# Big-head attention on one core: a wide subtraction as an entry of its own in the plan, and the statistics of three blocks one head earlier

## The reference, cut to what matters

```python
xn  = x / max(|x|, 1e-12) * sqrt(128) * gamma
q, k, v = split(xn @ w_qkv.T)            # 8 heads of width 128
sim = (q * 128**-0.5) @ k.T              # 2048 x 2048 for each head
sim = where(causal_mask, -max, sim)
out = softmax(sim) @ v                   # then @ w_out.T over all heads
x   = layernorm(x + out)
```

## Time and profile before

| | us |
|---|---|
| median of 3 runs | 1998.93 (1997.27 to 2002.44) |
| the profiled execution's own time | 2002.52 |
| its span | 2000.7 |
| TensorE busy | 1787.3 (89%) |
| VectorE busy | 1559.0 (78%) |
| ScalarE busy | 1374.9 (69%) |
| GpSimd busy | 419.6 (21%) |

### The profile page before, as it was taken

How to read it: one execution, slowest core, us unless ns; L and a number is a source line. 1 busy time by engine, 2 the same in 40 slices (tenths; PEclk the granted TensorE clock), 3 DMA queues, 4 the chain that set the end, 5 groups by cost and what they waited for, 6 DMA issues and landing times. The chain is left out here.

```text
span 2000.7 us, 40527 instructions
## 1 busy us (share of the span) xinstructions
PE 1787.3 (89%) x15880; PEld 958.9 (48%) x15880; DVE 1559.0 (78%) x2275; ACT 1374.9 (69%) x2569; POOL 419.6 (21%) x650
## 2 busy tenths in 40 slices
PE   6799999999999888849999999899679999998785
PEld 2122222222222278826888888789312322233384
DVE  5899999999999443547988788877578979785434
ACT  3499999999999743426665666566347998888331
POOL 4201000000000403343432221312320011122413
PEclk8599999999999988969999999999868999999597
DMA  5000000000000168700000000000100000000274
GB/s 171 1 3 4 4 11 3 4 11 4 4 11 5 34 220 279 243 21 1 1 1 1 1 1 1 1 1 1 55 1 2 5 4 11 5 12 7 67 264 154
DMA packets 52878, 81.57 MB, mean 41 GB/s; under 512 B 9200, under 2 KB 37744, under 8 KB 52560
## 3 DMA queue, kind: packets, MB, share of 16 engines
q1 hardware_dynamic: 47520, 70.50, 11.1%
q0 software_dynamic: 3072, 6.30, 1.0%
q10 hardware_dynamic: 2096, 2.17, 0.4%
HBM read 64.13 MB, written 12.06 MB: 38 GB/s over the span
## 5 line engine op out<-in xcount | busy, mean ns | idle before, releaser
L827 DVE TENSOR_REDUCE a_mx<-psum 128x2 f32<-128x1024 f32 (+2 forms) x832 | 906.0, 1154 | 75.3 <-PE psum L602 42.2
L753 ACT ACTIVATE a_cs<-psum 128x512 f32<-128x512 f32 (+3 forms) x1664 | 856.9, 571 | 80.7 <-PE psum L620 62.5
L643 PE MATMUL psum<-a_cs,a_V 128*16 128x256 f32 (+1 forms) x6400 | 501.7, 384 | 20.8 <-ACT a_OD L733 9.7
L602 PE MATMUL psum<-a_KS,a_QS 48*128 48x512 bf16 (+3 forms) x1664 | 328.7, 386 | 30.4 <-DVE a_mx L827 27.3
L620 PE MATMUL psum<-a_QS,a_KS 51*128 51x512 bf16 (+3 forms) x1664 | 336.8, 379 | 4.9 <-ACT a_cs L753 3.0
L620 PEld LDWEIGHTS psum<-a_QS,a_KS 51*128 51x128 bf16 x1664 | 87.8, 93 | 354.9 <-ACT a_cs L753 310.1
L2159 PE MATMUL psum<-b_VW,b_ST 128*128 128x129 f32 x2176 | 249.4, 276 | 0.3 <-DVE X L2291 0.3
L2159 PEld LDWEIGHTS psum<-b_VW,b_ST 128*128 128x128 f32 x2176 | 245.4, 192 | 0.5 <-DVE X L2291 0.5
L643 PEld LDWEIGHTS psum<-a_cs,a_V 128*16 128x16 f32 x6400 | 107.1, 94 | 245.1 <-issue 120.5
L2266 DVE TENSOR_TENSOR b_M<-b_M,b_ST 128x512 f32<-128x512 f32 (+3 forms) x264 | 158.1, 599 | 40.5 <-ACT b_ST L2198 11.8
L2203 ACT ACTIVATE b_ST<-b_ST 128x2048 f32<-128x2048 f32 x48 | 91.8, 1911 | 124.6 <-DVE b_ST L2274 124.6
(11 more groups left out here) (233 smaller groups left out, 1773.7 us busy)
## 6 DMA issues: line engine op xcount, KB each, us to landing
e_W<-in_l_experts SPq DMA_DIRECT2D x45, 576.0 KB, 5.8
e_W<-in_l_experts SPq DMA_DIRECT2D x21, 768.0 KB, 5.7
yg<-e_yout SPq DMA_DIRECT2D x14, 256.0 KB, 6.0
xg<-zeros SPq DMA_DIRECT2D x2, 1472.0 KB, 9.7
a_cs<-in_rope ACTq DMA_DIRECT2D x4, 512.0 KB, 10.0
a_QS<-a_mrow SPq DMA_DIRECT2D x128, 3.0 KB
a_cs<-in_rope SPq DMA_DIRECT2D x1, 2048.0 KB, 7.7
a_num<-a_OD SPq DMA_DIRECT2D x120, 16.0 KB
```

What stands on the lines that cost most here:

```text
L602: mm = pe.matmul(ps[:, 2 * slot + half, 0:width], QS[rows, 2 * p + i, q_cols(qb, qt * P, P)], KS[rows, 2 * p + i, c * BLK:c * BLK + width] ...
L643: mm = pe.matmul(ps[32 * j:32 * j + 2 * HD, AV_BANK, a:b], V[:, kt, HPP * p + j, :], probs(e, a, b), start=(kt == 0 and half == 0), stop=last,
L753: act.activation(probs(HPP * s + j, c, BLK), ps[:, plan.bank(entry), c:BLK], ACT.Exp, scale=scale).then_inc(exp_done, 1)
L827: dve.tensor_reduce(mx[:, pk % 2, qt, 2 * i:2 * i + 2, c], banks, AX.X, ALU.max).then_inc(max_done, 1)
```

## The change

`subtract` was one event for an atom, with all its wide and diagonal subtractions in a row. It becomes "narrow" events, one for each wide group and one for the four diagonal tiles, with due times 2.6 us apart. They stand in one sorted list, `timed`, with the exponentials. The first wide exponential is due 3.8 us behind the first subtraction, as before; each further one is now 2.6 instead of 2.3 us later. The diagonal exponentials were due at 1.5 + 2.3 (qb + 1) us (at least 4.0) and are now due 1.5 us behind the diagonal subtractions, at the earliest 0.1 us behind the last wide exponential. The statistics of the blocks 0 to 2 ("stats", VectorE) are due 10, 12 and 14 us behind the reduce of atom 26; "measure" stays for GpSimd's power, behind the reduce of atom 27.

```diff
-        self.clock, self.turns, self.spreads, self.norms, self.exps = 0.0, [], [], [], []
+        self.clock, self.turns, self.spreads, self.norms, self.timed = 0.0, [], [], [], []
...
         while self.norms and self.clock >= self.norms[0][0]:
             self.events.append(self.norms.pop(0)[1])
-        while self.exps and self.clock >= self.exps[0][0]:
-            self.events.append(self.exps.pop(0)[1])
+        self.due()
 
     def turn(self):
         _, a = self.turns.pop(0)
         self.events.append(("reduce", a))
+        if a == NORM_ATOM - 1:
+            behind = max(n for n, (qb, h) in enumerate(self.atoms) if qb in EARLY_BLOCKS)
+            self.norms = [(self.clock + 10.0 + 2 * n, ("stats", g, behind)) for n, g in enumerate(EARLY_BLOCKS)]
         if a == NORM_ATOM:
-            behind = max(n for n, (qb, h) in enumerate(self.atoms) if qb in EARLY_BLOCKS)
             for n, g in enumerate(EARLY_BLOCKS):
-                self.norms += [(self.clock + 0.5 + n, ("measure", g, behind)), (self.clock + (12.0, 14.0, 47.0)[n], ("normalize", g)),
+                self.norms += [(self.clock + 0.5 + n, ("measure", g)), (self.clock + (12.0, 14.0, 47.0)[n], ("normalize", g)),
                                (self.clock + (45.0, 48.0, 54.0)[n], ("fold", g))]
             self.norms.sort()
         self.spreads.append((self.clock + 4.5, a))
 
     def spread(self):
         _, a = self.spreads.pop(0)
-        self.events.append(("subtract", a))
         qb = self.atoms[a][0]
-        self.exps += [(self.clock + 1.5 + 2.3 * (g + 1), ("wide", a, g)) for g in range(qb)]
-        self.exps.append((self.clock + max(4.0, 1.5 + 2.3 * (qb + 1)), ("diagonal", a)))
+        for g in range(qb):
+            self.timed += [(self.clock + 2.6 * g, ("narrow", a, g)), (self.clock + 2.6 * g + 3.8, ("wide", a, g))]
+        behind = self.clock + 2.6 * qb
+        self.timed += [(behind, ("narrow", a, qb)), (max(behind + 1.5, self.clock + 2.6 * (qb - 1) + 3.9), ("diagonal", a))]
+        self.timed.sort()
+
+    def due(self):
+        while self.timed and self.clock >= self.timed[0][0]:
+            self.events.append(self.timed.pop(0)[1])
...
-            while self.exps and self.exps[0][1][1] <= a:
-                self.events.append(self.exps.pop(0)[1])
+            while any(event[1] <= a for _, event in self.timed):
+                self.events.append(self.timed.pop(0)[1])
...
-                def subtract(a):
+                def subtract(a, g):
                     qb = plan.atoms[a][0]
-                    dve.wait_ge(row_done, a + 1)
-                    dve.wait_ge(max_done, plan.max0[a + 1])
-                    for g in range(qb):
+                    if g == 0:
+                        dve.wait_ge(row_done, a + 1)
+                        dve.wait_ge(max_done, plan.max0[a + 1])
+                    if g < qb:
                         group = ST[:, plan.at[a][g], :, :]
                         dve.tensor_tensor(group, group, row[:, a % 2, :].unsqueeze(1).broadcast_to([P, TPB, BLK]),
                                           ALU.subtract).then_inc(wide_sub, 1)
+                        return
                     for i in range(TPB):
...
-                    elif event[0] == "subtract":
-                        subtract(event[1])
+                    elif event[0] == "narrow":
+                        subtract(event[1], event[2])
...
-                    elif event[0] == "measure":
+                    elif event[0] == "stats":
                         dve.wait_ge(added, 2 * (event[2] + 1))
                         norm.variance(dve, chain, event[1])
```

More of the change, by code:

```diff
@@ L1968, in lay @@
                     self.emit(("product", a, kt, half), 0.265 * len(self.columns(a, kt, half)))
-        assert not self.norms and not self.exps
+        assert not self.norms and not self.timed
         self.ring = [event for event in self.events if event[0] in ("query", "score", "fold")]
```

## The result

| | before | after |
|---|---|---|
| median, measured side by side (6 runs each) | 2001.18 (1997.27 to 2002.94) | 2010.88 (2004.58 to 2013.18) |
| ratio | | 1.0044, 95% interval 1.0029 to 1.0058 |
| the profiled execution's own time | 2002.52 | 2012.82 |
| its span | 2000.7 | 2011.0 |

The change makes the kernel 0.44% slower, 9.7 us in the medians. The forecast, +3.4 us, had the sign and not the size; 2010.88 lies 2.9 us above the top of the range, 2008.0. Of that, 2.3 us is that the kernel before came out at 2001.18 here and not at 1998.93; the rest is in the terms.

A forecast was written before the change was run, and what follows sets the result against it. TensorE was taken to wait for short VectorE instructions (b_GL) queued behind long ones; -0.6 - 0.3 + 2.9 - 2.0 + 3.4 = +3.4 us on 1998.93 gave a median of 2002.3, range 1993 to 2008.

The forecast's parts named there:

- term 4: Atoms 25 to 31: subtractions still fit before the next query, b_GL late by nothing; 0, at most 0.2 once or twice.
- term 3: Atom 24: b_GL comes 1.69 us earlier, the wait of 3.12 shrinks to 1.5; gain 2.0 us.
- Term 2: Atoms 18 to 23 (block 2): diagonal exponentials ahead of ScalarE's copy of tile 0 delay tile 5; 2.9 us slower.
- The rival with the full length: Block 2: tile 5 waits the exponentials' full 1.45 us all six times, 8.7 instead of 2.9; total 2008.1; chance 0.12.
- the one with nothing: Block 2: the exponentials cost nothing, term 2 is 0; total 1999.4 us; chance 0.16.
- Term 1: Small atoms: b_GL earlier by four diagonal subtractions, part lost to exponentials ahead of copies; gains 0.6 and 0.3 us.
- the 4.1: Small atoms: rest of the 5.5 us query wait, taken as no gain; rival that they give it: 1998.2, chance 0.08.
- Term 5: Statistics ahead of query 28: new wait of 5.2 us there, a second at query 29; 3.4 us slower.
- The clock part: Term 5: low granted clock behind the two new waits; 2.6 us slower if one has it, at most 4.8 if both.
- the statistics hide: Query 29: the wait of 6.11 falls to some 0.4 with its 2.2 of clock; total 1991.0 us; chance 0.10.
- the rival: GpSimd's power: part of its 7.49 us was a wait for statistics, so normalize's 1.9 wait goes; 2000.4; chance 0.12.

The follow-up runs named there:

- f7: The kernel after, unchanged, timed again in a later series: 2008.45 us, ratio 1.0022 to the kernel before.
- f6: The kernel after with the diagonal exponentials due as before in block 3 alone: 2007.40 us, ratio 1.0025 to the kernel before.
- f5: The kernel after with the diagonal exponentials due as before in block 2 alone: 2002.01 us, ratio 0.9997 to the kernel before.
- e4: The kernel before with only the new due times of the exponentials, subtractions one entry: 2003.08 us, ratio 1.0001.
- g4: The kernel before with only the new due times of the exponentials, timed a second time: 2003.70 us, ratio 1.0016.
- g5: The kernel after with diagonal exponentials and statistics back at their old places, leaving the split of the subtractions: 1998.72 us, ratio 0.9992 to the kernel before.
- e1: The kernel after with the diagonal exponentials alone back at their old due times: 2000.47 us, ratio 0.9990 to the kernel before.
- e2: The kernel after with the statistics alone back behind the reduce of atom 27: 2008.76 us, ratio 1.0033 to the kernel before.
- e3: The kernel before with the statistics alone moved to behind the reduce of atom 26: 2001.14 us, ratio 0.9994.
- g9: The kernel before with one statistics block in each all-reduce gap of atoms 25 to 27, normalize of blocks 0 and 1 in atom 28's: 1996.03 us, ratio 0.9972.

## Why the prediction was wrong

**The step that failed is term 4**, "b_GL was late by nothing there", put at 0 and measured at 3.8 us (27.70, and 27.65 in f7, for 23.90). b_GL was not late, but near it. For query 27 TensorE was due at its tile 4 at 1241.41 + 3.76 = 1245.17 before, and b_GL ran from 1243.78 for 0.68: 0.7 us of slack. I looked at the two parts of the change one at a time and priced each at nothing. Together they move b_GL from 11.48 to 13.13 us behind the reduce of atom 25 (12.41 with the exponentials alone, 11.70 with the split alone; 0.93 and 0.22 do not add up to the 1.65). And the gain of term 3 had brought query 27 from 9.1 to 8.3 us behind that reduce, which uses up slack as well. So 1.65 + 0.8 - 0.7 = 1.75 late; measured is a wait of 1.91, with 0.88 of granted clock over 1250 to 1260, together +3.8 us at query 28. The table of four shows that it takes both parts; the split alone has 1.1 of it. f6 shows what the other 2.7 are worth: 2.7 us at their place and nothing that can be measured in the whole, since VectorE's own bound takes most of it back one query on. By whole runs the dearer part is block 2, where the interval of f5 (0.9988 to 1.0005) lies under that of f7 (1.0008 to 1.0036).

**Term 2 had the mechanism, and its own atoms nearly the size; what lay beside them was in no term.** The segment has 4.0 for the 2.9 forecast. The atoms of the term, 18 to 23, put their exponentials behind queries 20 to 25. These queries are 18.89 apart instead of 18.37, 2.6 us for the five, and query 25 to 26 is 0.5 longer: 3.1 in all, the same as in e4 and g4. At 1137.80 tile 4 comes 4.34 behind its query instead of 4.26, and tile 5 1.09 behind tile 4 (1143.23) instead of 0.77 (1141.47 before): the copy of tile 0 is late as said, by 0.32 for the 0.44 forecast, and the longer wait for b_GL comes on top. The other 0.95 lie between query 19 and 20, behind atom 17, which no term has. There too the split puts an accumulate between the wide subtractions, and b_GL waits for GH, by 1.57 instead of 0.84; TensorE waits 0.66 for it here, 0.32 with the split alone and not at all before:

```profile
1085.05 0.69 DVE L2243 TENSOR_TENSOR b_GL<-psum,b_GH 128x512 fp32r<-128x512 f32 x1 [1.57 <-ACT b_GH L2190]
```

This stretch takes 17.60 before and with the exponentials alone, 18.22 with the split alone and 18.55 with both: what term 4 overlooked at atom 25 was overlooked here as well. f5 takes 3.4 of the 4.0 away. The rival with the full length, 8.7, is out, and so is the one with nothing. That f5's median gains 6.4 on f7's where the segments show 4.2 stays open; the part outside the stage varies by more than that from one profile to another.

**Term 1 was right on the split and wrong on the exponentials.** The split alone is worth 2.1 us in the small atoms (g5 and e1), more than the 0.9 taken: of the 4.1 that I had put down to VectorE's total, some is to be had. The early diagonal exponentials cost 3 us there (e1 and g5 against e2, f5 and f6). The main place of it is ahead of query 3, where TensorE now waits 1.36 for ScalarE's copy of the values: query 2 to 3 takes 11.08 in all seven kernels with the diagonal exponentials late and 12.31 to 14.00 in the seven profiles with them early, of which the next stretch gives 0.35 back. I had counted only the scores' copies behind them.

**Term 3 was right**: 2.2 for 2.0, the wait 1.65 for 1.5, and the granted clock of 1220 to 1230 is 1.00.

**Term 5 had its waits, and no price.** The profile after has all of its parts: the statistics between the subtractions of atom 26, the b_GL of query 28 behind them, and normalize held up by GpSimd's power, 1.59 for a forecast of 1.9:

```profile
1266.97 0.86 DVE L942 BATCH_NORM_STATS2 b1n_stats<-X 128x6 f32<-128x128 f32 x4
...
1276.30 0.68 DVE L2243 TENSOR_TENSOR b_GL<-psum,b_GH 128x512 fp32r<-128x512 f32 x1
...
1300.88 1.12 DVE L1836 TENSOR_SCALAR big_raw<-X,b1n_mv,b1n_scales 128x128 f32<-128x128 f32 x4 [1.59 <-POOL b1n_scales L1826]
```

The wait at query 28 is 3.07 and not 5.2 only because TensorE was already held up at query 27: where that wait is gone (e1, f6) it is 5.2. The second is 2.38, for 2.4 to 3.1. In e3, which has the move alone, VectorE takes 56.44 us from the b_GL of query 27 to that of query 29 (1242.61 to 1299.05) instead of 54.81 (1243.78 to 1298.59): +1.6 for +2.6. The clock part had the wrong sign. I had two waits cost as much clock as one or more; the last segment of e3 is 1.0 us shorter than before, with 0.97 of granted clock over 1260 to 1320 against 0.94:

```profile
1260.00:1320.00 60.00, 54.08 (x372) 48.89 (x371) 51.56 (x102) 36.24 (x51) 14.34 (x14) 0.97 0.00 1
```

So the statistics' term was near 0, and its rival "the statistics hide" wrong too in the way it was put; that hiding pays was shown in another place, by g9 (5.4 us in that segment, normalize's move included). That the segment's +2.4 lies near the +3.4 forecast is luck: 1.1 of it stands behind query 31, where the split costs it and no term had anything.

**The idle time of GpSimd ahead of the power** is 7.07 us here against 7.49 in the earlier trace rows, though the last statistics had now been ready for 16 us when GpSimd took the power up at 1291.8 (1275.65). Over the 14 profiles it is 6.64 to 7.70, with the statistics early (6.64 to 7.70) as with them right behind the reduce (6.83 to 7.49). It is thus no wait for them, as I had held against the rival, and with normalize's wait of 1.59 the rival is out:

```profile
1298.90 3.56 POOL L1826 TENSOR_TENSOR b1n_scales<-b1n_both,b1n_half 128x8 f32<-128x8 f32 x2 [7.07 <-issue]
```

By sums: forecast -0.9 + 2.9 - 2.0 + 0 + 3.4 = +3.4, measured in the stage +0.4 + 4.0 - 2.2 + 3.8 + 2.4 = +8.5. What stays open is how the rest of the +2.4 behind query 28, beyond the 1.1 at its end, is shared by the statistics, the exponentials and the split, since a wait removed at one query came back at the next (0.36 for 1.91 at query 27 in f6, then 5.21 for 3.1) and the granted clock behind query 28 differs from trace to trace: the same kernel had 125.30 us there at 0.96 of full clock and 123.45 at 0.99.

## What to carry to other kernels

Take "hidden" for a number of microseconds, not for a yes: write the slack beside each term that is put at 0, and take it off again for what every other term of the same change uses up, its gains included. Work that must go somewhere belongs where its engine already waits for another (here VectorE for the all-reduce, 1.92 us), measured against the length of that gap. And an order that helps where TensorE waits for one short instruction (atoms up to 24) can hurt where the reordered engine is itself the bound (the split alone gave 2.7 us at query 27 and took 2.3 behind query 28), so set it stage by stage.

## What the hardware showed beyond the forecast

The gap of 1.92 us in which VectorE waits for the all-reduce took the 2.1 us of statistics while the subtraction moved by about 0.1 (in g9 the maxima end at 1228.79, and it starts at 1230.82, 2.03 behind them). One instruction of the statistics is longer beside an all-reduce: over the 14 profiles L1818 takes 0.67 to 0.68 in each of the 14 places where it overlaps one and 0.17 in each of the other 28. GpSimd's masks, too, differ in length at one shape (128x128): L2087 takes 0.29 to 1.43 us over the 128 of them in the kernel before, the longest at 946.20 beside subtractions of VectorE. Why was not tested in either case. The time outside the stage, with the same instructions in the same order, spread over 8.7 us from profile to profile. And a wait of 1.36 ahead of query 3 was once followed by six matmuls in 2.84 us and once by four in 3.67, on the same kernel:

```profile
911.55 2.84 PE L2134 MATMUL psum<-big_raw,AT 128*128 128x512 f32 x6 [1.36 <-ACT b_VW L2197]
```

```profile
912.21 3.67 PE L2134 MATMUL psum<-big_raw,AT 128*128 128x512 f32 x4 [1.36 <-ACT b_VW L2197]
```

(the kernel after in its first trace, and in f7's). Of the seven profiles with the diagonal exponentials early, two have 12.31 us from query 2 to 3 and five 13.8 to 14.0. What decides between the two was not tested.
